# Spreading gathers and group loads over time in a two-layer attention kernel

## The reference

```
xn = LN(x)
s  = attention(xn)            # layer 0: linear attention (elu features); layer 1: causal softmax, 16 heads, values of width 32
g  = silu(ffn(xn))            # layer 0: causal softmax attention, then a mixture of 8 experts, top 2; layer 1: one linear map with LoRA
x  = x + s * g
```

```
scores = (q_r @ k_r.T + q_i @ k_i.T) / 4 ; probs = softmax(causal(scores)) ; out = (probs @ v) @ Wo
```

## Time and profile before

| | us |
|---|---|
| median of 3 runs (lowest, highest) | 3001.39 (2997.93, 3002.08) |
| the profiled execution, its own time | 3008.54 |
| span of the profiled execution | 3006.4 |
| PE busy in the span | 2831.9 (94%) |
| DVE, ACT, POOL busy | 2010.2, 1545.3, 990.0 |
| PE busy in the second attention, 1960 to 3006 | 1005.10 of 1046.00 |
| mean granted PE clock | 0.969 of full speed |

### The profile page before, as it was taken

The page is one execution under the profiler, slowest core; times in us unless marked ns, Lnnn a source line. Parts: engine busy times, 40 slices in busy tenths (PEclk is TensorE's granted clock), DMA queues, the critical chain, the costliest instruction groups (busy, mean ns, idle before and its releaser), DMA issues. The chain is left out here.

```text
span 3006.4 us, 46248 instructions
## 1 busy us (share of the span) xinstructions
PE 2831.9 (94%) x18017; PEld 1317.3 (44%) x18017; DVE 2010.2 (67%) x4329; ACT 1545.3 (51%) x2581; POOL 990.0 (33%) x533
## 2 busy tenths in 40 slices
PE   7998999999999976999999899899999999999999
PEld 4664233333333344666676545323333333333327
DVE  7887899999999845000000565688787877878823
ACT  3452477676777755222222444345565665565571
POOL 1000000110101103111101330157777777777791
PEclk9997899999999987999999999889999999999999
DMA  4322122133202124232111466312020220202103
GB/s 130 97 77 76 37 51 39 43 62 66 50 24 62 24 68 130 63 86 75 63 48 34 148 193 185 79 32 61 8 64 12 68 64 8 64 12 68 67 12 119
DMA packets 141306, 200.77 MB, mean 67 GB/s; under 512 B 14320, under 2 KB 107904, under 8 KB 138000
## 3 DMA queue, kind: packets, MB, share of 16 engines
q1 hardware_dynamic: 130672, 173.21, 20.9%
q0 software_dynamic: 9056, 24.59, 3.9%
q10 hardware_dynamic: 1360, 0.01, 0.0%
HBM read 121.21 MB, written 76.02 MB: 66 GB/s over the span
## 5 line engine op out<-in xcount | busy, mean ns | idle before, releaser
L946 ACT ACTIVATE at_probs<-at_st 128x512 f32<-128x512 f32 (+3 forms) x1280 | 588.5, 542 | 442.1 <-PE at_st L1040 282.4
L909 POOL TENSOR_TENSOR at_probs<-at_probs 128x2048 f32<-128x2048 f32 (+3 forms) x205 | 725.9, 3546 | 214.7 <-ACT at_probs L946 135.4
L393 DVE TENSOR_REDUCE at_part<-at_s 128x1 f32<-128x512 f32 (+3 forms) x1280 | 690.0, 603 | 63.0 <-PE at_s L431 28.6
L368 ACT ACTIVATE at_probs<-at_st 128x1024 f32<-128x1024 f32 (+3 forms) x640 | 541.6, 895 | 275.4 <-PE at_st L450 141.0
L972 DVE TENSOR_REDUCE at_part<-at_s 128x1 f32<-128x512 f32 x768 | 498.5, 683 | 67.8 <-PE at_s L1032 63.9
L966 DVE CUSTOM_DVE_ANT_0 at_s<-at_s,at_later 128x384 f32<-128x384 f32 (+3 forms) x512 | 246.9, 498 | 103.8 <-PE at_s L1032 102.4
L510 PE MATMUL at_acc<-at_probs,at_v 128*32 128x512 f32 (+3 forms) x2560 | 305.5, 551 | 8.2 <-ACT at_otile L355 7.8
L2358 DVE TENSOR_TENSOR ex_ot<-ex_bank,lin_b 128x512 f32<-128x512 f32 x32 | 22.2, 692 | 426.3 <-PE ex_bank L2388 352.2
L2321 ACT ACTIVATE ex_hT<-ex_bank,ex_b 128x512 f32<-128x512 f32 x128 | 87.9, 687 | 334.7 <-PE ex_bank L2378 332.7
L2378 PE MATMUL ex_bank<-ex_xT,lin_w 128*128 128x512 f32 x512 | 225.5, 598 | 1.0 <-ACT ex_xT L2314 1.0
L2388 PE MATMUL ex_bank<-lin_w,ex_hT 128*128 128x256 f32 x1024 | 223.7, 379 | 0.8 <-ACT ex_hT L2321 0.8
(11 more groups left out here) (342 smaller groups left out, 3950.0 us busy)
## 6 DMA issues: line engine op xcount, KB each, us to landing
att<-at_otile SPq DMA_DIRECT2D x64, 256.0 KB, 2.1
lin_w<-in_W SPq DMA_DIRECT2D x16, 1024.0 KB, 7.5
at_v<-v SPq DMA_DIRECT2D x11, 1024.0 KB, 11.1
v<-pr_vt SPq DMA_DIRECT2D x32, 256.0 KB
exp_out<-ex_ot SPq DMA_DIRECT2D x32, 256.0 KB, 2.1
v<-p_vt SPq DMA_DIRECT2D x32, 256.0 KB, 3.7
p_xs<-in_x SPq DMA_DIRECT2D x8, 512.0 KB, 5.2
qhi<-p_parts SPq DMA_DIRECT2D x8, 512.0 KB
```

The lines of the kernel that those rows point to most:

```text
L368: act.activation(probs[:, quad % RING, heads_down * p:heads_down * (p + 1), off:QB], st_ps[n % st_slots][:, :, off:QB], ACT.Exp, scale=EXP ...
L393: dve.tensor_reduce(part[:, w % 2, qt * HG + h, j:j + 1], s_ps[n % S_SLOTS][:, 0:width], AX.X, ALU.max).then_inc(item_free, 1)
L909: pool.tensor_tensor(total, total, probs[:, slots.slot[quad], :, off:QB], ALU.add).then_inc(add_done, 1)
L946: act.activation(probs[:, slots.slot[quad], h, off:QB], st_ps[n % ST_SLOTS][:, off:QB], ACT.Exp, scale=EXP_SCALE).then_inc(exp_done, 1)
```

## The change

It has five parts. (1) Experts: the gathers for expert 1 wait until PE has done `h03 0` and `h07 0`. (2) Opening of the last projection: tile n's gathers wait for a later step of PE: tile 0 for none, tiles 1 to 10 for `nT n+n//2`, tile 11 for T 0, tiles 12 to 31 each for one of qB, kB, vB, y of the round before the one in which the tile is mixed. (3) Same stage: silu 0 comes after s 7 in place of s 9, sqrt 0 after s 10 in place of s 12, and on DVE x 0, moments 0 and z 0 come before the rest of mixed 1; SP's loads of x and the weights come a step earlier. (4) `load_group`'s 11 DMAs are given out in 8 parts between the stores of rounds 4, 5 and 6. (5) Second attention: a group's load, now 8 DMAs with v in two halves, is given out one for every fourth ST, and so is `load_finish`; the planner's constant for the earliest S of group g+2 goes from 12000 to 24000 ns.

```diff
-                    ready = max(ready, pv_end[last_of[g - 2]] + 12000)
+                    ready = max(ready, pv_end[last_of[g - 2]] + 24000)
...
-        def load(eng, g):
+        def load(eng, g, n):
             k = g % 2
-            for dst, src, r in ((QT, q_hi, 0), (KT, k_hi, 0), (QT, q_lo, 1), (KT, k_hi, 1), (QT, q_hi, 2), (KT, k_lo, 2)):
-                eng.dma_start(dst[k][r * hd:(r + 1) * hd, :, :],
-                              src[g].rearrange("h d t -> d h t")).then_inc(qk_ld[k], 16)
-            eng.dma_start(V[k][:, :, :], v[g]).then_inc(v_ld[k], 16)
+            if n < 6:
+                r = n // 2
+                dst, src = (QT, KT)[n % 2], (q_hi, k_hi, q_lo, k_hi, q_hi, k_lo)[n]
+                eng.dma_start(dst[k][r * hd:(r + 1) * hd, :, :], src[g].rearrange("h d t -> d h t")).then_inc(qk_ld[k], 16)
+            else:
+                part = slice(NKC // 2 * (n - 6), NKC // 2 * (n - 5))
+                eng.dma_start(V[k][:, part, :], v[g][:, part, :]).then_inc(v_ld[k], 16)
...
+                elif ev[0] == "ST":
+                    pairs += 1
+                    if pairs % EVERY == 0 and group:
+                        if loaded < (LOADS if group < GROUPS else Carried.FINISH_PARTS):
+                            sp.wait_ge(st_ready, pairs)
+                            if group < GROUPS:
+                                load(sp, group, loaded)
...
-            for e, cb in ((0, 1), (1, 0), (1, 1)):
-                gather_tokens(pool, z_rows, rows_at, xin, rows_ld, e, cb)
+            gather_tokens(pool, z_rows, rows_at, xin, rows_ld, 0, 1)
+            for cb, f in ((0, half - 1), (1, NFF - 1)):
+                pe_s.wait(pool, f"h0{f} 0")
+                gather_tokens(pool, z_rows, rows_at, xin, rows_ld, 1, cb)
...
+    GROUP_AT = {(4, "q"): 1, (4, "k"): 1, (4, "v"): 1, (5, "q"): 1, (5, "k"): 1, (5, "v"): 1, (6, "q"): 2}
...
-    act_after = {9: ["silu 0"], 12: ["sqrt 0"], 15: ["silu 1"]}
+    act_after = {7: ["silu 0"], 10: ["sqrt 0"], 15: ["silu 1"]}
...
-            pe_s.wait(sp, "s 4")
+            pe_s.wait(sp, "s 3")
             load_x(0)
             for n, name in enumerate(("Wq", "Wk", "Wv")):
-                pe_s.wait(sp, f"s {2 * n + 6}")
+                pe_s.wait(sp, f"s {2 * n + 5}")
...
                 if b >= 2:
                     dve_s.wait(pool, f"mixed {b - 2}")
-                else:
-                    pe_s.wait(pool, f"nT {n + 1}")
+                if 0 < n < 12:
+                    pe_s.wait(pool, f"nT {n + n // 2}" if n < 11 else "T 0")
+                elif n:
+                    pe_s.wait(pool, f"{('qB', 'kB', 'vB', 'y')[t]} {b - 3}")
...
             mixed(0)
+            combine(0)
+            statistics(0)
             mixed_tile(1, 0)
             mixed_tile(1, 1)
-            combine(0)
-            statistics(0)
+            normalised(0)
             mixed_tile(1, 2)
             mixed_tile(1, 3)
-            normalised(0)
```

More of the change, by code:

```diff
@@ L738, in __init__, with load_group @@
                   for t in (self.q, self.k) for y in range(2)]
-    def load_group(self, eng, C, qk, v):
+    def load_group(self, eng, C, qk, v, n):
         K = 32
[L742 to L748, removed]
+        if n < 6:
+            dst, src = (self.q, self.k)[n % 2], (qk[0][0], qk[1][0], qk[0][1], qk[1][0], qk[0][0], qk[1][1])[n]
+            eng.dma_start(dst[n // 2 * K:(n // 2 + 1) * K, :, :], src[0].rearrange("h d t -> d h t")).then_inc(self.group_ld, 16)
+        elif n == 6:
+            for h in range(HG):
+                eng.dma_start(self.k[3 * K:3 * K + 2, h, :], C["shift_rows"][2 * h:2 * h + 2, h, :]
+                              ).then_inc(self.group_ld, 16)
+        else:
+            eng.dma_start(self.v[:, :, :], v[0, 0]).then_inc(self.group_ld, 16)
+    GROUP_PARTS = 8
     GROUP_LOADS = 11 * 16
@@ L755, in load_value, with load_finish @@
                       ).then_inc(self.a_ld[k], 16)
[L757 to L760, removed]
+    FINISH_PARTS = 1 + NQB
+    def load_finish(self, eng, W, att, n):
+        if n:
+            self.load_value(eng, att, n - 1)
+        else:
+            eng.dma_start(self.w, W["Wo"].rearrange("(g p) n -> p g n", p=P)).then_inc(self.w_ld, 16)
 def wide_attention(nc, tag, C, q_hi, q_lo, k_hi, k_lo, v, out, W, carried, turned, share, x_all, g_all, result):
@@ L841, in _ @@
             ended, issued = [], [0, 0]
+            pairs = group = loaded = 0
             def store(unit):
@@ L864, in _ @@
                     if w == 1:
[L865 to L870, removed]
-                    elif g + 2 == GROUPS:
-                        sp.wait_ge(pv_done, quads_done[ev[1]])
+                        group, loaded = 1, 0
+                elif ev[0] == "EV" and ev[1] == last_unit[ev[1][0]] and ev[1][0] + 2 <= GROUPS:
+                    while group < GROUPS and loaded < LOADS:
+                        load(sp, group, loaded)
+                        loaded += 1
+                    group, loaded = ev[1][0] + 2, 0
+                    sp.wait_ge(pv_done, quads_done[ev[1]])
+                    if group == GROUPS:
                         for k in range(2):
                             sp.wait_ge(out_stored[k], issued[k])
-                        carried.load_finish(sp, W, out)
+                elif ev[0] == "ST":
[4 more added lines that the diff above has]
+                            if group < GROUPS:
+                                load(sp, group, loaded)
+                            else:
+                                carried.load_finish(sp, W, out, loaded)
+                            loaded += 1
+            assert group == GROUPS and loaded == Carried.FINISH_PARTS
             while ended:
@@ L2515, in _ @@
             load_x(1)
-            pe_s.wait(sp, "s 12")
+            pe_s.wait(sp, "s 13")
             sp.dma_start(bias[:, :], W["bias"].unsqueeze(0).to_broadcast([P, D])).then_inc(w_ld[1], 16)
@@ L2526, in _ @@
                     sp.wait_ge(v_kept, 64 * NQB)
-                    carried.load_group(sp, C, qk_out, v_out)
+                    group = 0
                 for side, name in enumerate("qk"):
@@ L2533, in _ @@
                                      parts[:, side, lower, :, :]).then_inc(part_out, 16)
+                    for _ in range(GROUP_AT.get((b, name), 0)):
+                        carried.load_group(sp, C, qk_out, v_out, group)
+                        group += 1
                 act_s.wait(sp, f"vB {b}")
@@ L2536, in _ @@
                     sp.dma_start(v_out[s, g, :, 4 * j:4 * j + 4, :], vt[:, :, g * P:(g + 1) * P]).then_inc(v_kept, 16)
+                for _ in range(GROUP_AT.get((b, "v"), 0)):
+                    carried.load_group(sp, C, qk_out, v_out, group)
+                    group += 1
             sp.wait_ge(part_out, 64 * NB)
```

11 lines of the change are left out of this document (7 added, 4 removed).

## The result

The changed kernel took 3008.53 us (median of 9 runs, 3002.86 to 3010.99) and the kernel before 3001.14 us (9 runs, 2997.27 to 3003.78). The ratio is 1.0027, interval 1.0018 to 1.0036: slower by 0.27%, where 2990.6 us and a gain of 0.36% were forecast. The profiled execution of the changed kernel took 3010.9 us, its span is 3009.2.

What follows compares the result with a forecast made beforehand. PE, busy 94%, bounds the kernel; its waits in the last projection's opening were to go. The opening's 14.4 us, other terms 0, gave a median of 2987.0 to 2994.2, middle 2990.6 us (-0.36%), range 2984 to 3003.

Steps and rivals of the forecast that it cites:

- The opening's term: Opening of the last projection: without ACT and SP seeing PE's steps late (the hold-up), T 0 comes 14.4 us earlier.
- The rival that spaced gathers still hold signals up: Opening: half of the stall stays, half of 10.7 us is won, 2996 us; chance 0.07.
- the sum: Whole kernel: 14.4 us off the profiled execution; median falls 7.2 to 14.4 us, middle taken, 2990.6 us.
- The rival "made by the recording": Opening: recording PE's instructions makes the hold-up, so unrecorded runs win nothing, 3001.4 us; chance 0.20.
- The rival "the fourth tile comes late": Rounds 1 to 5: the fourth tile's gather lands 3.5 us over its slack in each, 3008 us; chance 0.06.
- The fourth tile's upper end: One round with parts of group 0 ahead of the fourth tile's gather: tile 4 us late, once; taken as 0.
- The slack of 1.1 us: Last projection's rounds: DVE leaves 5.5 us for the fourth tile's gather, which needs 4.4 to issue and land; cost 0.
- Costs taken as 0: Gathers in the rounds, expert 1's held gathers, group 0 in parts and the second attention's parted loads: 0 us each.
- The rival that parted loads win: Second attention: unrecorded executions wait longer for loads than the trace's 2.2 us, so under 2984 us; chance 0.04.
- the likeliest case: Whole kernel: the forecast gain of 7 to 14.4 us, 2985 to 2996 us; chance 0.60.

Runs made afterwards that it cites:

- the five jobs near 3015: Follow-up jobs 1, 2, 3, 4 and 6, in which the unedited kernel before had medians of 3015.2, 3014.0, 3017.6, 3015.0 and 3017.1 us.
- the first comparison: The study's main measurement, changed kernel against the kernel before: 3008.5 us beside 3001.1 us.
- job 5: Follow-up job on chip 13: kernel before, unedited, against itself, 3001.0 beside 2999.1 us; the changed kernel there 3008.7 us, ratio 1.0028.
- jobs 4 and 5: Two follow-up jobs, both on chip 13; the unedited kernel before took 3015.0 us in one and 2999.1 us in the other.
- the one with quarters: Kernel before with only the opening's edits, plus POOL's multiplication of attention rows in four quarter pieces: 3000.6 us beside 3017.6 for the kernel before, 0.9948.
- one word: Changed kernel with the fourth tile's gather waiting for vB in place of y, against the kernel before: 3001.5 us (0.9963), then 2998.0 us (0.9937).

## Why the prediction was wrong

**The opening's term, as a reading of the trace: right.** T 0 was to come 14.4 us earlier and came 14.17. Spacing is what did it, the burst what made it; ACT, SP and PE had no other wait. The rival that spaced gathers still hold signals up is out.

**The step that failed: the sum.** "The median of the runs that were not recorded is 7.15 us lower", and I took the middle of 7.2 and 14.4. The premise was that one execution and three runs of the same kernel differ by the recording. They differ by the job: the profiled execution had the hold-up, as the five jobs near 3015 have it (three of them by a profile), and the runs of the first comparison stand where job 5 stands, which has none. That those runs had none is inferred from their time, since none of those nine has a profile here. In such a job the opening wins 0.0 us, not 10.7. The 7.15 us did not bound the hold-up either. Its size is 13 to 18 between jobs and 14 to 17 in profiles. Against the profile of the same kernel in job 5 the profiled execution had 14.2 us more to T 0, but 3.4 less ahead of the stage (its first 1129 us are near the early end of 1128 to 1136 in 18 profiles of identical code there), 1.4 less from T 0 to the second attention and 1.6 less behind: 7.8 in all. So a hold-up of 14 us looked like 7.

**The rival "made by the recording"** gave the right result for that term, nothing won, by a wrong mechanism: job 5 has a recorded execution of before without the hold-up. The rule of the Trainium skill that was set beside it (NOTIFIC — the notification-queue block, 7.1 Overflow), that the path of the records can throttle an engine, does not decide here, since recorded executions came out with and without the hold-up, and whole jobs of unrecorded ones at either level.

**The rival "the fourth tile comes late"** gave 3008, as measured, and that is luck: it took 3.5 us in each of five rounds, 17.5, off a gain of 10.7. The runs show 4.9 to 6.4 in one round and under 1 in the others, and no gain to take it off.

**The fourth tile's upper end: the second failure.** The bound of 4 us, once, in the round where parts of group 0 lie ahead, named the round and the mechanism; I took 0, and 4.9 to 6.4 us came, in four profiles of the changed kernel. The bound counted PE's idle piece (3.1 to 3.8 more) and not the low clock behind it (1.5 to 2.9). The reason I gave for 0, that engines kept their round beside those loads, was read in a kernel whose gathers had been issued long ahead. The slack of 1.1 us was about right for the other rounds (0.15 us lost in each). By the Trainium skill (DMA: Bandwidth & Descriptors, Queues, rings and completion order) the gather would not stand behind SP's whole backlog, and the upper end would be near 0. The trace disagrees with that end: the gather was there 6.7 us after its issue, with a DMA share of 1.11 and 0.97 meanwhile, against 1.9 at the opening. And issued just ahead of q's part (1814.1 and 1815.3 for 1815.8), it cost nothing. How the engines take turns within those 6.7 us no run here shows.

**Costs taken as 0.** The parts of the second attention, those of group 0 by themselves, and the held gathers of expert 1 (from the experts' first matmul to the last projection the profiles have 465.2 us before and 465.3 after) cost nothing, as forecast. The rival that parted loads win has nothing for it.

**Together.** In a job without the hold-up: 0 won and 7.1 lost, +7.1; measured +7.4 in the first comparison and +9.6 in job 5 (+7.8 against that job's own twelve runs of before). In a job with it: -13 to -18 + 7 = -6 to -11, measured -7.4 and -9.4, whose 3006.6 and 3008.1 are still outside the likeliest case. The forecast missed the time by 18 us: 10.7 of a gain that was not there, and 7 of a loss taken as 0.

**Open.** What makes a job have the hold-up or not, on one and the same chip, and what it is that keeps PE's steps from ACT and SP. No run here showed the placement of buffers or anything else that differs between jobs 4 and 5.

## What to carry to other kernels

When the profiled execution and the timed runs of one kernel differ by more than the runs do among themselves, treat a stall in that profile as one that may not be in the timed runs at all, and take the case without it at full weight. A gather moved from long ahead to just in time gets the price of the worst round beside it, the low clock behind PE's idle piece included. Issue it a step earlier, ahead of the transfers that it must not queue behind: one word did that here and kept the gain, in two jobs that had one to keep.

## What the hardware showed

- 24 gathers at 1.25 us each, beside PE's steps of 2.16 us, held up PE's steps for ACT and SP by up to 13 us in some jobs and not at all in job 5. With 3.2 us from tile to tile no profile in any job has the hold-up; with 2.7 all but 3.9 us of it were gone.
- A lower granted clock cost as much as a wait. y 0 took 5.41 us in the 13 profiles whose opening took 37.8 to 39.1 us, and 3.72 in that of the kernel before, after idle pieces that were alike (2.15 and 2.12 us). It goes either way where the opening is longer: 5.41 with 52.3 and 50.9 us, 3.72 with 52.1, 51.9 and 41.7. In the changed kernel the clock there was 0.72 from 1709 to 1715:

```profile
1709.45 5.41 PE L2821 MATMUL p_bank<-p_w_ffn,p_xT 128*128 128x256 f32 x16 [2.15 <-DVE p_parts L2718]
```

```profile
1709.00:1715.00 6.00, 5.55 (x17) 4.48 (x18) 0.50 (x2) 3.28 (x4) 0.37 (x1) 0.72 0.87 283
```

- The stretch ahead of the experts, the same code in all kernels but the one with quarters, differs by up to 8 us between executions, in steps of 1 to 3 us: some where the granted clock differs, some where small instructions of DVE meet POOL's multiplications. Windows at 413 us of the kernel before and of the one with quarters, whose own edit first runs at 467:

```profile
413.00:420.00 7.00, 6.89 (x58) 2.21 (x62) 6.46 (x13) 5.90 (x8) 0.00 (x0) 1.00 0.78 116
```

```profile
413.00:420.00 7.00, 6.89 (x45) 1.76 (x42) 5.83 (x12) 5.01 (x6) 0.00 (x0) 0.83 0.56 91
```

- DVE's small instructions waited for POOL's whole multiplication. The Trainium skill (SBUF — State Buffer, Who interferes with whom) says that the port pair which the two share is a lock held for a whole instruction; the trace agrees, 1.20 us of wait and work beside POOL's 1.2 us pieces, and 0.38 beside its quarters of 0.45 us.
